# The gate of a recurrent block, computed by pairs of tokens

## The chip, the cores and the metric

One core of one Trainium2 chip runs the whole program. The metric is the time of one execution on the device in microseconds (us).

## The reference, cut to what matters

The input x has 4 sequences of 1024 tokens and 512 features. Four layers follow each other, each adding its result to x; all is fp32. The third layer is the one that changes:

```
x = x + L0(x)          # two-layer MLP with an expert's rows, hidden size 2048
x = x + L1(x)          # 512 x 512 weight picked per sequence
# L2
ctx[t]  = a * ctx[t-1] + x[t]                       # causal average, a is one number
wg      = sigmoid([x, ctx] @ Wg.T + bg)             # Wg = [W1, W2], each 512 x 512
gated   = x * wg
mod     = 0.5 + sigmoid(gelu(x @ Wn1.T + bn1) @ Wn2.T + bn2)        # 4 columns
traces  = causal averages of gated * mod[d], d = 0..3
gate    = sigmoid(sum_d(traces[d] * blend[d]) @ Wtemp.T + btemp)
soma    = gelu(x @ Wsoma.T + bsoma)
x = x + layernorm((soma * gate) @ Wout.T) * gamma + beta
x = x + L3(x)          # 512 x 512 weight picked per sequence
```

## The kernel before, in words

The tokens are cut into 8 tiles of 512 (two per sequence, t or i = 0..7), the features into 4 chunks of 128 partitions (c or m = 0..3). A tile lies with its features on the partitions and its tokens along them. Each fp32 operand of TensorE (PE) is split into a high part (rounded to fp32r by an ACT copy) and a low part (the rest, by a DVE subtraction); a product is three fp32r matmuls, hi x hi, hi x lo and lo x hi (`split_product`, L1441 to L1443), each with a weight load of its own.

The work has two halves. **The first half** (layers 0 and 1) goes by pairs p = 0..3 of tiles. In a unit (p, k), k = 0..7, the first matrix of the MLP is multiplied by seven Strassen products (P1, P5, P6, P2, P7, P4, P3 on PE, in this order), with fc2 products of earlier blocks between them. Products P1, P6, P7 and P4 share a bank: ACT copies it out after P1, P6 and P7 (`p1_of`, `u2_of` at L972, `u3_of`), and P7 waits for `u2_of`. At unit 1 the second tile of the pair before passes through layer 1, and in unit 2 DVE makes its low parts (`x2_lo`). After the eight units the second tile of the pair has 16 fc2 steps, j = 0..15; the hidden blocks come back from DRAM (`hb_lo`, `w2_lo` make their low parts). The 37 pieces of the later weights are split on the way and parked in DRAM. The result x2 of a tile is stored as fp32 and as its two parts.

**The second half** (layers 2 and 3) goes by tiles i. PE's order in round r from 2 on is: N1(r), the first gate block (r,0) with the small product MO(r) inside, TE of tile r-1 (four blocks), gates (r,1) and (r,2), L3 of tile r-2 (four blocks, in round 7 two), gate (r,3), OU of tile r-1, SO(r), with SS(r-1) between. Tile 0's gates lie between the last fc2 steps of the first half (after j = 4, 7, 10, 13), and in round 1 the gates (1,1), (1,2), (1,3) follow one another, since no L3 is ready.

A gate block (i, m) sums over eight products: because gate[t] - a gate[t-1] = (W1 + W2) x[t] - a W1 x[t-1], each chunk gives one product with W1 + W2 and one with -a W1 and the tokens moved by one (the tile is loaded behind a halo of one token, `LEAD`). DVE then runs the recurrence over the bank (`scan_g`, L2078), ACT takes the tanh (`wg_tanh`), and DVE makes `gated`, four drives, four traces and their sum (`traces_a` to `traces_d`) and its low part (`temporal_low`), which TE needs in the next round. The gate weights, 1 MB for each m, are loaded once and stay (`wg_hl[0..3]`).

Each engine runs an instruction list written out by hand; waits are on semaphores, and nothing is reordered. Loads and stores are issued from SP's queue, some from ACT's and POOL's, in the order of the code.

Of the kernel before, what the change touches and what calls it, by code (L numbers as in the profile page):

```python
# [23 lines left out]
SLOTS = 6  # L24

# [16 lines left out]
def build(nc, x, tok16, tok8, small, fc1_w, fc2_w, exp_w, exp_b, l1_w, l1_b, wg, wn1, wsoma, wtemp, wout,  # L42
# [15 lines left out]
    with ctx:  # L58
# [12 lines left out]
        def sem(name):  # L71
# [38 lines left out]
        mod_row = place("mod_row", 4, [TOK])  # L110

        LEAD = 64
        SLOT_KIB = 2 * (LEAD + TOK) * 4 / KIB
        x2_slot = [place(f"x2_slot{s}", 6 + SLOT_KIB * s if s < 4 else 112 + SLOT_KIB * (s - 4), [2, LEAD + TOK], F32R)
                   for s in range(SLOTS)]
        gated = place("gated", 24, [TOK])
        drive = [place(f"drive{s}", 26 + 2 * s, [TOK]) for s in range(2)]
        sumsq = place("sumsq", 30, [TOK])
        sumsq_lo = place("sumsq_lo", 30, [TOK], F32R)
        h1_hi = place("h1_hi", 30, [TOK], F32R)  # L120
        wg_hl = [place(f"wg_hl{m}", at, [2 * KC, 2, P], F32R) for m, at in enumerate((32, 56, 64, 72))]
        mod_t = place("mod_t", 40, [TAUS, TOK])
        temporal = place("temporal", 160, [KC, TOK])
        temporal_lo = place("temporal_lo", 160, [KC, TOK], F32R)
        wsoma_hl = place("wsoma_hl", 80, [KC, 2, DIM], F32R)
# [10 lines left out]
        l3w_at = (152, 156, 200, 121)  # L136
        l3w_hl = [place(f"l3w_hl{c}", at, [2, DIM], F32R) for c, at in enumerate(l3w_at)]

        l3w_last = [place(f"l3w_last{c}", at, [2, DIM], F32R) for c, at in enumerate((32, 36, 56, 60))]
        o_late = place("o_late", 64, [KC, TOK])  # L140
        x3_hi_late = place("x3_hi_late", 64, [KC, TOK], F32R)
        sq_late = place("sq_late", 72, [KC, TOK])
        spikes_hi_late = place("spikes_hi_late", 80, [KC, TOK], F32R)
        y_sb = [place("y_sb0", 125, [TOK]), place("y_sb1", 4, [TOK])]

        wn2_hl = place("wn2_hl", 127, [2, P], F32R)
# [10 lines left out]
        alpha_minus = const("alpha_minus", 1)  # L157
# [6 lines left out]
        zeros = const("zeros", 2)  # L164
        ones = const("ones", P, F32R)
        ident = const("ident", P)
# [40 lines left out]
        s_wg = [sem(f"s_wg{m}") for m in range(KC)]  # L207
# [18 lines left out]
        s_halo = [sem(f"s_halo{c}") for c in range(KC)]  # L226
        s_zero = sem("s_zero")
        s_last_hi = sem("s_last_hi")
        s_slot = [sem(f"s_slot{s}") for s in range(SLOTS)]
        s_xt = [sem(f"s_xt{s}") for s in range(3)]  # L230
# [6 lines left out]
                ("L1", "N1", "SO", "MO", "WG", "TE", "OU", "SS", "L3")}  # L237
# [154 lines left out]
        MADE = [p for p, (k, _) in enumerate(PARKED) if k in ("WG", "OU", "L3")]  # L392


        parked_units = ((4, 5, 6, 7, K8 + 3, K8 + 6, K8 + 9, K8 + 12),
                        (1, 2, 3, 5, 6, K8 + 4, K8 + 8, K8 + 12),
# [18 lines left out]
        for c in range(0, 2 * KC, 2):  # L415
            p = PARKED.index(("WG", c))
            assert parked_number[p + 1] == parked_number[p] + 1
# [51 lines left out]

        def x2_at(i, c):  # L470
            return (KC * i + c) % SLOTS
# [42 lines left out]
        def _(eng):  # L514
# [67 lines left out]
            def load_stage(n):  # L582
# [4 lines left out]
                else:  # L587
# [5 lines left out]
                    elif k == "WG":  # L593
                        source = wg[:, c // 2 if c % 2 else KC + c // 2, :]
# [9 lines left out]
            def parked(k, c):  # L604
# [3 lines left out]
                return parked_dram(p).rearrange("a p n -> p a n")  # L608
# [5 lines left out]
            def load_wg(m):  # L614
                if m:
# [4 lines left out]
                parked("WG", 2 * KC - 1)  # L620
                eng.dma_start(wg_hl[m].bitcast(F32).rearrange("p k a n -> p (k a) n"),
                              wg_dram[:, :, :, m * P:(m + 1) * P].rearrange("k a p n -> p (k a) n")
                              ).then_inc(s_wg[m], 16)

            def load_wsoma(c):
                if c < 2:
                    on.wait_ge(s_x2st, 16 * LAST)
                    on.wait_ge(s_x2lo, KC * LAST)
                on.wait_ge(s_stlo, STAGED)
                on.wait_ge(s_pstlo, 16 * len(PARKED))  # L630
                for row in range(2):
                    on.wait_ge(s_hbst[row], 16 * K8 * PAIRS)
# [10 lines left out]
            def load_x(t):  # L643
                if t >= 2:
                    on.wait_ge(s_x2st, 16 * (t - 1))
                    on.wait_ge(s_x2lo, KC * (t - 1))
# [12 lines left out]

            def load_xt(i):  # L660
# [4 lines left out]
                elif i == 2:  # L665
                    on.wait_ge(s_x2lo, KC * NT)
# [5 lines left out]
            def load_slot(i, c):  # L672
                if i == 0:
                    on.wait_ge(s_prod, prod_no(PAIRS - 1, K8 - 1, ("P6", "P2", "P7", "P4")[c]) + 1)
                elif c < 2:
                    if i > 1:
                        on.wait_ge(s_pe["SO"], KC * (i - 1))
                    else:
                        on.wait_ge(s_fc2, UNITS)
# [6 lines left out]
                if i % HALVES:  # L686
                    on.wait_ge(s_halo[c], 16 * (i // HALVES + 1))
                else:
                    on.wait_ge(s_zero, 16 * KC * B)
                s = x2_at(i, c)  # L690

                if c == KC - 1 and i > 1:
                    eng.dma_start(x2_slot[s][:, 0, LEAD - 1:].bitcast(F32), x2hl_dram[i, c, :, 0, :]).then_inc(s_last_hi, 16)
                    eng.dma_start(x2_slot[s][:, 1, LEAD - 1:].bitcast(F32), x2hl_dram[i, c, :, 1, :]).then_inc(s_slot[s], 16)
                else:
                    eng.dma_start(x2_slot[s][:, :, LEAD - 1:].bitcast(F32), x2hl_dram[i, c]).then_inc(s_slot[s], 16)

            def load_l3w(b):
                for c in range(KC):
                    if b == B - 1:  # L700
                        on.wait_ge(s_pe["WG"], KC * LAST + 1 + c // 2)
# [5 lines left out]
                    else:  # L707
                        on.wait_ge(s_fc2, UNITS)
                    eng.dma_start(l3w_of_tile(HALVES * b, c)[:, :, :].bitcast(F32), parked("L3", KC * b + c)).then_inc(s_l3w[c], 16)
# [23 lines left out]
            for p in range(PAIRS):  # L733
                for k in range(K8):
# [5 lines left out]
                    if p and k == 2:  # L740
                        store_x2(HALVES * p - 2)
                    if p and k == 4:
                        store_x2(HALVES * p - 1)
                    if k in (5, 6):
                        load_x(HALVES * p + k - 5)
# [3 lines left out]
                    if k == K8 - 1 and p == PAIRS - 1:  # L749
# [3 lines left out]
                        for c in range(1, KC):  # L753
                            load_slot(0, c)
                    store_hb(p, k, 1)
# [8 lines left out]
                for j in range(HC if p < PAIRS - 1 else 0):  # L764
                    pass_staged(p, K8 + j)
                    if j in (4, 8):
# [11 lines left out]
            uses_done(4)  # L778
            load_wg(2)
# [1795 lines left out]
```

## Time and profile before

| | |
|---|---|
| median of 2 runs | 1317.53 us (1317.52 to 1317.55) |
| profiled execution | 1317.3 us, of which the span of the trace is 1315.6 |
| PE | 1306.4 us busy, 5725 matmuls |
| DVE | 1033.5 us busy |
| ACT | 668.5 us busy |
| DMA | 196.57 MB, 149 GB/s on average |

The span is the time from the first to the last instruction of the program in the trace. PE's busy time counts a matmul from its start to a modelled end, and successive ones overlap: it tells that PE is hardly ever without work, not how fast it works. The time of a matmul in a stream is read from a stretch: its length divided by the matmuls that start in it.

### The profile page before, as it was taken

The numbers are of one execution on the slowest core, as the hardware profiler recorded it, in microseconds if no ns is written. First come the engines' busy times: TensorE is split into PE (matmuls) and PEld (weight loads), VectorE is DVE, ScalarE is ACT, GpSimd is POOL, SyncE is SP. The second block draws the span as 40 slices with busy tenths as digits, with TensorE's granted clock in tenths as the row PEclk, the third lists the DMA queues.
The fourth block names the chain that finished last, engine by engine and source line by source line (L and its number), as shares of the span: only waits on it lengthen the run. The fifth ranks groups of instructions, "written<-read, shape, count | busy, mean of one in ns | idle before, by whom it ended". The sixth has DMA issues, their size and how long they took to land.

```text
span 1315.6 us, 16412 instructions
## 1 busy us (share of the span) xinstructions
PE 1306.4 (99%) x5725; PEld 1072.1 (81%) x5725; DVE 1033.5 (79%) x1635; ACT 668.5 (51%) x1237; POOL 102.1 (8%) x135
## 2 busy tenths in 40 slices
PE   9999999999999999999999999999999999999998
PEld 7788888888888888888887887788888888888877
DVE  7876786767778768676644898999898889897974
ACT  6576475765466664566643322434334353535254
POOL 0010010030000000100000100013000210021000
PEclk9999999999999999999999999999999999999999
DMA  8256563766445766636667567512132123312101
GB/s 289 97 179 230 168 176 121 231 169 202 139 135 189 233 214 194 167 102 222 229 216 212 175 205 198 186 41 88 65 130 95 65 97 128 97 65 97 49 16 64
DMA packets 102122, 196.57 MB, mean 149 GB/s; under 512 B 9704, under 2 KB 28136, under 8 KB 98968
## 3 DMA queue, kind: packets, MB, share of 16 engines
q1 hardware_dynamic: 84608, 154.99, 37.1%
q10 hardware_dynamic: 11576, 24.70, 6.1%
q0 software_dynamic: 5856, 15.83, 3.9%
q8 instruction: 46, 0.75, 0.2%
q14 instruction: 36, 0.29, 0.1%
HBM read 125.65 MB, written 69.83 MB: 149 GB/s over the span
## 4 chain that ended last, share of the span: by engine, by line
PE 92%; DVE 5%; ACT 1%; issue 1%; DMA 0%; ACTq 0%; DVEq 0%
PE bank L1441 31%; PE bank L1442 30%; PE bank L1443 30%; DVE drive L2115 1%; DVE drive L2102 1%; DVE temporal L2130 0%; DVE t_lo L1876 0%; DMA x_raw<-in_x 0%; DVE temporal L2115 0%; DVE bank L2078 0%; ACT x_hl L1043 0%; DVE sp_hl L1876 0%; DVE t_raw L1905 0%; DVE w_hl L1876 0%; ACT bank L983 0%
## 5 line engine op out<-in xcount | busy, mean ns | idle before, releaser
L1441 PE MATMUL bank<-h_hl,w_hl 128*128 128x512 f32 x512 | 199.5, 390 | 0.0
L1443 PE MATMUL bank<-h_hl,w_hl 128*128 128x512 f32 x512 | 199.3, 389 | 0.0
L1442 PE MATMUL bank<-h_hl,w_hl 128*128 128x512 f32 x512 | 199.2, 389 | 0.0
L1441 PE MATMUL bank<-t_hi,sp_hl 128*128 128x512 f32 x448 | 175.3, 391 | 3.7 <-DVE t_lo L1876 1.2
L1442 PE MATMUL bank<-t_lo,sp_hl 128*128 128x512 f32 x448 | 174.4, 389 | 0.0
L1443 PE MATMUL bank<-t_hi,sp_hl 128*128 128x512 f32 x448 | 174.3, 389 | 0.0
L1441 PEld LDWEIGHTS bank<-h_hl,w_hl 128*128 128x128 f32 x512 | 96.1, 188 | 20.9 <-issue 0.8
L1443 PEld LDWEIGHTS bank<-h_hl,w_hl 128*128 128x128 f32 x512 | 96.1, 188 | 20.0
L1442 PEld LDWEIGHTS bank<-h_hl,w_hl 128*128 128x128 f32 x512 | 96.1, 188 | 19.8
L1441 PEld LDWEIGHTS bank<-t_hi,sp_hl 128*128 128x128 f32 x448 | 84.1, 188 | 24.4 <-issue 1.8
L1441 PE MATMUL bank<-x_slot,wg_hl 128*128 128x512 f32 x256 | 100.6, 393 | 0.0
L1442 PE MATMUL bank<-x_slot,wg_hl 128*128 128x512 f32 x256 | 99.8, 390 | 0.0
L1443 PE MATMUL bank<-x_slot,wg_hl 128*128 128x512 f32 x256 | 99.4, 388 | 0.0
L1443 PEld LDWEIGHTS bank<-t_hi,sp_hl 128*128 128x128 f32 x448 | 84.1, 188 | 17.5
L1442 PEld LDWEIGHTS bank<-t_lo,sp_hl 128*128 128x128 f32 x448 | 84.1, 188 | 17.2
L2102 DVE SCALAR_TENSOR_TENSOR drive<-gated,small_sb,mod_t 128x512 f32<-128x512 f32 x128 | 92.1, 740 | 3.7 <-issue 2.1
L1876 DVE TENSOR_TENSOR w_hl<-w_raw,w_hl 128x512 fp32r<-128x512 f32 x128 | 86.8, 686 | 6.5 <-ACT w_hl L959 5.4
L1026 ACT ACTIVATE h_hl<-hb_in 128x512 fp32r<-128x512 f32 x64 | 40.2, 628 | 87.3 <-DMA hb_in<-hb_dram 44.9
L959 ACT ACTIVATE w_hl<-w_raw 128x512 fp32r<-128x512 f32 x128 | 78.4, 620 | 6.3 <-PE bank L1443 6.3
L1876 DVE TENSOR_TENSOR h_hl<-hb_in,h_hl 128x512 fp32r<-128x512 f32 x64 | 44.0, 688 | 38.5 <-ACT h_hl L1026 38.5
L943 ACT ACTIVATE sp_hl<-s_raw_sb 128x256 fp32r<-128x256 f32 x128 | 50.9, 411 | 39.5 <-PE bank L1443 38.0
L2130 DVE TENSOR_TENSOR temporal<-drive,temporal 128x512 f32<-128x512 f32 x96 | 66.0, 687 | 1.0
(225 smaller groups left out, 2824.3 us busy)
## 6 DMA issues: line engine op xcount, KB each, us to landing
fc_raw<-in_fc_w SPq DMA_DIRECT2D x32, 512.0 KB, 4.2
hb_dram<-hb_out SPq DMA_DIRECT2D x64, 256.0 KB, 2.6
hb_in<-hb_dram ACTq DMA_DIRECT2D x64, 256.0 KB, 3.3
x2hl_dram<-x_hl POOLq DMA_DIRECT2D x28, 512.0 KB, 7.1
x_slot<-x2hl_dram SPq DMA_DIRECT2D x26, 513.0 KB, 5.1
stage<-in_l_w SPq DMA_DIRECT2D x32, 256.0 KB, 3.5
x_raw<-in_x SPq DMA_DIRECT2D x8, 1024.0 KB, 6.3
x_dram<-x_raw SPq DMA_DIRECT2D x8, 1024.0 KB, 8.1
```

Source lines behind the costliest of these rows:

```text
L943: eng.activation(sp_hl[n % RING][:, 0, :, :], product_source(n), ACT.Copy).then_inc(s_shi, 1)
L959: eng.activation(w2_hl[v % 3][:, 0, :, :], w2_raw[:, j, :, :], ACT.Copy).then_inc(s_w2hi, 1)
L1026: eng.activation(h_hl[v % 4][:, 0, :], hb_in[v % 4][:, :], ACT.Copy).then_inc(s_hhi, 1)
L1441: eng.matmul(ps, w_hi, x_hi, start=first, stop=False, skip_group_check=resumed)
L1442: eng.matmul(ps, w_hi, x_lo, start=False, stop=False, skip_group_check=resumed)
L1443: return eng.matmul(ps, w_lo, x_hi, start=False, stop=final, skip_group_check=resumed)
L1876: return eng.tensor_tensor(lo, raw, hi.bitcast(F32), ALU.subtract)
L2102: eng.scalar_tensor_tensor(drive[d % 2][:, :], gated[:, :], blend_sb[:, TAUS * c + d:TAUS * c + d + 1], mod_t[:, d, :], ALU.mult, ALU.mult ...
L2115: eng.tensor_tensor_scan(traced, alpha[:, 1 + d:2 + d].to_broadcast([P, TOK]), drive[d % 2][:, :], start, ALU.mult, ALU.add).then_inc(s_tr ...
L2130: eng.tensor_tensor(temporal[:, c, :], drive[d % 2][:, :], temporal[:, c, :], ALU.add).then_inc(s_add, 1)
```

## The change

The gate is computed by pairs of tokens 2k and 2k+1. With q[k] = W2 ctx[2k], the even token is W1 x[2k] + q[k], and the odd one (W1 + W2) x[2k+1] + a q[k]. A block is three products for each chunk, on 256 columns: q, even tokens, odd tokens, the moving operand taking every second word of a tile. The context is made by DVE scans in place over x2 and split into parts by ACT and DVE, and stored; for tiles 0 to 5 this lies in units 2 to 6 of the pair after, for tile 6 in steps j = 12 to 15, for tile 7 in round 1. ACT copies q out twice, once times a (`q_of`), and DVE adds it to the bank (`gate_sum`) where the scan was. The gate weights have 12 pieces (1.5 MB for each m) and two buffers: each block's weights are loaded anew, from block 6 on by ACT behind the tanh of two blocks earlier. The halo is gone. Tile 0's gates now lie after j = 4, 8, 11, 14. The places of tiles in SBUF and banks, and some waits, are moved to suit.

```diff
-        wg_hl = [place(f"wg_hl{m}", at, [2 * KC, 2, P], F32R) for m, at in enumerate((32, 56, 64, 72))]
+        wg_hl = [place(f"wg_hl{g}", at, [3 * KC, 2, P], F32R) for g, at in enumerate((28, 68))]
-        PARKED += [("WG", c) for c in range(2 * KC)]
-        PARKED += [("OU", c) for c in range(KC)] + [("L3", c) for c in range(B * KC)]
+        PARKED += [("WG", c) for c in range(3)] + [("OU", 0)] + [("WG", c) for c in range(3, 3 * KC)]
+        PARKED += [("OU", c) for c in range(1, KC)] + [("L3", c) for c in range(B * KC)]
...
+        def q_bank(i, m):
+            b, half = (((6, 1), (0, 0), (1, 0), (3, 0)) if i else ((6, 1), (4, 0), (5, 0), (4, 1)))[m]
+            return bank[b][:, PAIR * half:PAIR * (half + 1)]
...
+                if k == "WG":
+                    eng.dma_start(wg_dram[:, :, c, 0, :].rearrange("m p n -> p m n"),
+                                  stage_hi[:, :].bitcast(F32).rearrange("p (m n) -> p m n", n=P)).then_inc(s_psthi, 16)
...
+            def store_ctx(t):
+                on.wait_ge(s_ctxlo, KC * (t + 1))
+                eng.dma_start(ctx_dram[t], x_raw[t % 2][:, :, :]).then_inc(s_ctxst, 16)
...
+            def load_ctx(i, c):
+                if i:
+                    on.wait_ge(s_pe["WG"], KC * i)
...
+            def ctx_hi(t, c):
+                on.wait_ge(s_ctx, KC * t + c + 1)
+                if t % HALVES == 0:
+                    eng.activation(g_last[:, c:c + 1], x_raw[t % 2][:, c, TOK - 1:TOK], ACT.Copy).then_inc(s_glast, 1)
+                    on.wait_ge(s_glast, KC * (t // HALVES) + c + 1)
+                xc = pairs(x_raw[t % 2][:, c, :])
+                eng.activation(xc[:, :, 1].bitcast(F32R), xc[:, :, 0], ACT.Copy).then_inc(s_ctxhi, 1)
...
+            def q_of(i, m):
+                n = KC * i + m
+                on.wait_ge(s_pe["Q"], n + 1)
+                on.wait_ge(s_g, n)
+                eng.activation(q_sb[:, 0:PAIR], q_bank(i, m), ACT.Copy)
+                eng.activation(q_sb[:, PAIR:], q_bank(i, m), ACT.Copy, scale=alpha[:, 0:1]).then_inc(s_q, 1)
+
             def wg_tanh(i, m):
                 ps = wg_bank(i, m)
                 on.wait_ge(s_g, KC * i + m + 1)
...
                 eng.activation(ps[:, :], ps[:, :], ACT.Tanh, bias=bg_sb[:, m:m + 1], scale=0.5
                                ).then_inc(s_wgt, 1)
+                g = KC * i + m + 2
+                if 6 <= g < KC * NT:
+                    on.wait_ge(s_pe["WG"], g - 1)
+                    eng.dma_start(wg_hl[g % 2][:, :, :, :].bitcast(F32), wg_dram[g % KC]).then_inc(s_wg[g % 2], 16)
...
+            contexts_at = {3: (0, 0), 4: (0, 2), 5: (1, 0), 6: (1, 2)}
             def unit(p, k):                       # ACT
...
                     h_of_c12(p, k - 1)
                     staged_hi(p, k - 1, late=True)
+                    if p and k in contexts_at:
+                        ctx_hi(t - 1 + contexts_at[k][0], contexts_at[k][1])
+                        ctx_hi(t - 1 + contexts_at[k][0], contexts_at[k][1] + 1)
...
-                on.wait_ge(s_wg[m], 16)
+                g = KC * i + m
+                w = wg_hl[g % 2]
+                on.wait_ge(s_wg[g % 2], 16 * (g // 2 + 1))
+                if i == 0:
+                    on.wait_ge(s_x2 if m else s_x1, KC * LAST)
+                    if m == 3:
+                        on.wait_ge(s_q, 2)
+                elif m:
+                    on.wait_ge(s_spk, KC * (i - 1) + (1, 2, 4)[m - 1])
+                else:
+                    on.wait_ge(s_gated, KC * (i - 1) + (3 if i > 1 else 4))
+                if m == 0 and i:
+                    gate_tokens(i, m, 0, 1)
+                    if i == 2:
+                        mo(i)
+                on.wait_ge(s_cslot, 16 * KC * (i + 1))
+                for c in range(KC):
+                    mm = split_product(q_bank(i, m), w[:, 3 * c + 2, 0, :], w[:, 3 * c + 2, 1, :],
+                                       ctx_slot[c][:, :, 1], ctx_slot[c][:, :, 0], c == 0, c == KC - 1)
+                mm.then_inc(s_pe["Q"], 1)
+                if m == 0 and i > 2:
+                    mo(i)
+                if m or not i:
+                    gate_tokens(i, m, 0, 1)
+                gate_tokens(i, m, 1, 0).then_inc(s_pe["WG"], 1)
+
+            def gate_tokens(i, m, token, part):
+                w = wg_hl[(KC * i + m) % 2]
                 for c in range(KC):
                     x2 = slot(i, c)
-                    for k, before in ((2 * c, 0), (2 * c + 1, 1)):
-                        at = LEAD - before
-                        mm = split_product(wg_bank(i, m)[:, :], wg_hl[m][:, k, 0, :], wg_hl[m][:, k, 1, :],
-                                           x2[:, 0, at:at + TOK],
-                                           x2[:, 1, at:at + TOK], c == 0 and not before,
-                                           c == KC - 1 and before == 1)
+                    mm = split_product(wg_bank(i, m)[:, PAIR * token:PAIR * (token + 1)], w[:, 3 * c + part, 0, :],
+                                       w[:, 3 * c + part, 1, :], pairs(x2[:, 0, :])[:, :, token], pairs(x2[:, 1, :])[:, :, token],
+                                       c == 0, c == KC - 1)
+                return mm
...
+            def context(t, c):
+                start = 0.0
+                on.wait_ge(s_x2st, 16 * (t + 1))
+                on.wait_ge(s_x2lo, KC * t + c + 1)
...
+                xr = x_raw[t % 2][:, c, :]
+                eng.tensor_tensor_scan(xr, alpha[:, 0:1].to_broadcast([P, TOK]), xr, start, ALU.mult, ALU.add
+                                       ).then_inc(s_ctx, 1)
+            def context_lo(t, c):
+                on.wait_ge(s_ctxhi, KC * t + c + 1)
+                xc = pairs(x_raw[t % 2][:, c, :])
+                low_part(xc[:, :, 0].bitcast(F32R), xc[:, :, 0], xc[:, :, 1]).then_inc(s_ctxlo, 1)
-            def scan_g(i, m):
...
+            def gate_sum(i, m):
+                ps = wg_bank(i, m)
                 on.wait_ge(s_pe["WG"], KC * i + m + 1)
+                on.wait_ge(s_q, KC * i + m + 1)
+                eng.tensor_tensor(ps[:, :], ps[:, :], q_sb[:, :], ALU.add).then_inc(s_g, 1)
...
+            contexts_at = {2: (0, 0), 3: (0, 2), 4: (1, 0), 5: (1, 2)}
             def unit(p, k):                       # DVE
...
                 staged_lo(p, k)
+                if p and k - 1 in contexts_at:
+                    context_lo(t - 1 + contexts_at[k - 1][0], contexts_at[k - 1][1])
+                    context_lo(t - 1 + contexts_at[k - 1][0], contexts_at[k - 1][1] + 1)
...
                 staged_made(p, k, late=True)
+                if p and k in contexts_at:
+                    context(t - 1 + contexts_at[k][0], contexts_at[k][1])
+                    context(t - 1 + contexts_at[k][0], contexts_at[k][1] + 1)
...
                     if j == 12:
+                        context(LAST - 1, 0)
+                        context(LAST - 1, 1)
                         traces_a(0, 1)
                     if j == 13:
+                        context(LAST - 1, 2)
+                        context(LAST - 1, 3)
                         traces_b(0, 1)
                     if j == 14:
+                        context_lo(LAST - 1, 0)
+                        context_lo(LAST - 1, 1)
                         traces_c(0, 1)
+                        gate_sum(0, 2)
+                    if j == 15:
+                        context_lo(LAST - 1, 2)
+                        context_lo(LAST - 1, 3)
                         traces_d(0, 1)
...
             spikes_low(0, 2, 2)
+            context(LAST, 0)
+            context(LAST, 1)
             traces_d(1, 0)
-            scan_g(1, 1)
+            gate_sum(1, 1)
```

## Rows read from the trace of the kernel before

**Rows 1.** The page, part 1: busy us (share of the span) and instructions by engine.

```profile
PE 1306.4 (99%) x5725; PEld 1072.1 (81%) x5725; DVE 1033.5 (79%) x1635; ACT 668.5 (51%) x1237; POOL 102.1 (8%) x135
```

**Rows 2.** Stretches: length, then PE, PEld, DVE, ACT, POOL busy, PEclk, DMA, GB/s.

```profile
730.00:860.00 130.00, 129.50 (x561) 104.15 (x560) 122.32 (x169) 44.10 (x76) 5.83 (x9) 1.00 0.62 184
...
1058.25:1127.65 69.40, 69.40 (x306) 57.23 (x305) 62.43 (x76) 28.62 (x45) 0.71 (x1) 1.00 0.31 106
```

**Rows 3.** Stretches, PE alone: three gate blocks; two SO blocks.

```profile
809.65:826.11 16.46, 16.46 (x73) 1.00 0.99 185
...
837.01:842.45 5.44, 5.44 (x25) 1.00 0.01 3
```

**Rows 4.** Weight loads: timeline of the warm-up (start, length), and lines (busy, mean ns).

```profile
1.21 3.70 PEld L1751 LDWEIGHTS bank<-ones 128*128 128x128 f32 x17 [1.21 <-DVE eps_sb L2205]
...
5.10 0.53 PEld L1751 LDWEIGHTS bank<-ones 128*128 128x128 f32 x4
...
L1442 PEld LDWEIGHTS bank<-x_slot,wg_hl 128*128 128x128 f32 x256 | 48.0, 188 | 10.0
```

**Rows 5.** Lines by form, DVE and ACT: count, busy us, mean ns, idle before.

```profile
L2078 DVE TENSOR_TENSOR_SCAN bank<-alpha,g_last,bank 128x512 f32<-128x512 f32 x16 | 20.5, 1283 | 4.3 <-PE bank L1443 4.3
...
L1952 DVE TENSOR_TENSOR bank<-bank,p_sb 128x512 f32<-128x512 f32 x28 | 19.6, 698 | 21.6 <-PE bank L1443 21.6
...
L2115 DVE TENSOR_TENSOR_SCAN drive<-alpha,drive 128x512 f32<-128x512 f32 x48 | 58.1, 1210 | 0.0
...
L1876 DVE TENSOR_TENSOR sp_hl<-s_raw_sb,sp_hl 128x256 fp32r<-128x256 f32 x128 | 52.3, 420 | 17.5 <-ACT sp_hl L943 17.5
...
L943 ACT ACTIVATE sp_hl<-s_raw_sb 128x256 fp32r<-128x256 f32 x128 | 50.9, 411 | 39.5 <-PE bank L1443 38.0 <-DVE s_raw_sb L1919 1.3
```

**Rows 6.** Timeline (start us, us) of pair 3, unit 3 and the start of unit 4.

```profile
606.26 2.49 DVE L1876 TENSOR_TENSOR x_hl<-x_raw,x_hl 128x512 fp32r<-128x512 f32 x4
...
608.61 0.60 ACT L972 ACTIVATE u_sb<-bank 128x512 f32<-128x512 f32 x1 [0.38 <-PE bank L1443]
...
609.77 0.39 PE L1441 MATMUL bank<-t_hi,sp_hl 128*128 128x512 f32 x1
...
620.02 0.68 DVE L1876 TENSOR_TENSOR w_hl<-w_raw,w_hl 128x512 fp32r<-128x512 f32 x1
...
623.57 0.60 ACT L972 ACTIVATE u_sb<-bank 128x512 f32<-128x512 f32 x1 [0.38 <-PE bank L1443]
```

**Rows 7.** Timeline (start us, us) from step j = 14 to the start of TE(1).

```profile
757.88 0.69 DVE L1876 TENSOR_TENSOR w_hl<-w_raw,w_hl 128x512 fp32r<-128x512 f32 x1
...
762.11 0.40 PE L1441 MATMUL bank<-h_hl,w_hl 128*128 128x512 f32 x1
...
798.77 0.39 PE L1441 MATMUL bank<-ts_hi,wtemp_hl 128*128 128x512 f32 x1
...
820.78 1.29 DVE L2078 TENSOR_TENSOR_SCAN bank<-alpha,g_last,bank 128x512 f32<-128x512 f32 x1
...
826.12 0.40 PE L1441 MATMUL bank<-ts_hi,wout_hl 128*128 128x512 f32 x1
...
857.50 2.35 DVE L1876 TENSOR_TENSOR temporal_lo<-temporal,ts_hi 128x1024 fp32r<-128x1024 f32 x2
...
858.86 0.47 PE L1441 MATMUL bank<-ts_hi,wtemp_hl 128*128 128x512 f32 x1 [0.17 <-DVE temporal_lo L1876]
```

**Rows 8.** DMA issues of the whole span: count, KB each, median us to landing.

```profile
xt<-x_dram SPq DMA_DIRECT2D x8, 1024.0 KB, 5.8
```

**Rows 9.** Timeline (start us, us) of round 6, and of round 7 to TE(7).

```profile
1151.20 1.28 DVE L2165 SCALAR_TENSOR_TENSOR soma<-bank,soma 128x512 f32<-128x512 f32 x2
...
1224.96 1.28 DVE L2078 TENSOR_TENSOR_SCAN bank<-alpha,g_last,bank 128x512 f32<-128x512 f32 x1
...
1262.77 2.35 DVE L1876 TENSOR_TENSOR temporal_lo<-temporal,ts_hi 128x1024 fp32r<-128x1024 f32 x2
...
1264.59 0.39 PE L1441 MATMUL bank<-ts_hi,wtemp_hl 128*128 128x512 f32 x1
```

More of the change, by code:

```diff
@@ L206, in build @@
         s_wn1 = sem("s_wn1")
-        s_wg = [sem(f"s_wg{m}") for m in range(KC)]
+        s_wg = [sem(f"s_wg{g}") for g in range(2)]
         s_wsoma = sem("s_wsoma")
@@ L225, in build @@
         s_hl7 = [sem(f"s_hl7{c}") for c in range(KC)]
[L226 to L227 removed]
+        s_ctx = sem("s_ctx")
+        s_ctxhi = sem("s_ctxhi")
+        s_ctxlo = sem("s_ctxlo")
+        s_ctxst = sem("s_ctxst")
         s_last_hi = sem("s_last_hi")
         s_slot = [sem(f"s_slot{s}") for s in range(SLOTS)]
+        s_cslot = sem("s_cslot")
+        s_q = sem("s_q")
         s_xt = [sem(f"s_xt{s}") for s in range(3)]
@@ L414, in build @@
         STAGED = len(staging)
-        for c in range(0, 2 * KC, 2):
+        for c in range(0, 3 * KC, 3):
             p = PARKED.index(("WG", c))
@@ L619, in load_wg @@
                     on.wait_ge(s_prod, prod_no(PAIRS - 1, K8 - 1, "P6") + 1)
[L620 to L623, printed above, removed]
+                was_parked("WG", 3 * KC - 1)
+                eng.dma_start(wg_hl[g % 2][:, :, :, :].bitcast(F32), wg_dram[g % KC]).then_inc(s_wg[g % 2], 16)
             def load_wsoma(c):
[L626 to L632, printed above, removed]
+                on.wait_ge(s_w2lo, UNITS - HC + 2 * c + 2)
                 eng.dma_start(wsoma_hl[:, c, :, :].bitcast(F32), parked("SO", c)).then_inc(s_wsoma, 16)
@@ L678, in load_slot @@
                     else:
-                        on.wait_ge(s_fc2, UNITS)
+                        on.wait_ge(s_ctxst, 16 * LAST)
+                        for row in range(2):
+                            on.wait_ge(s_hbst[row], 16 * K8 * PAIRS)
+                        on.wait_ge(s_prod, len(PRODUCTS))
                 else:
@@ L708, in load_l3w @@
                         on.wait_ge(s_fc2, UNITS)
+                        on.wait_ge(s_stlo, STAGED)
+                        on.wait_ge(s_pstlo, 16 * len(PARKED))
+                        for row in range(2):
+                            on.wait_ge(s_hbst[row], 16 * K8 * PAIRS)
                     eng.dma_start(l3w_of_tile(HALVES * b, c)[:, :, :].bitcast(F32), parked("L3", KC * b + c)).then_inc(s_l3w[c], 16)
@@ L752, in _ @@
                         load_wg(0)
-                        for c in range(1, KC):
+                        for c in (1, 3, 2):
                             load_slot(0, c)
+                        for c in range(KC):
+                            load_ctx(0, c)
                     store_hb(p, k, 1)
@@ L823, in _ @@
                 if r + 1 < NT:
+                    for c in range(KC):
+                        load_ctx(r + 1, c)
                     load_slot(r + 1, 2)
@@ L1348, in _ @@
                 spikes_hi(0, m)
+            ctx_hi(LAST, 0)
+            ctx_hi(LAST, 1)
+            q_of(1, 1)
             wg_tanh(1, 1)
+            ctx_hi(LAST, 2)
+            ctx_hi(LAST, 3)
+            q_of(1, 2)
             wg_tanh(1, 2)
+            q_of(1, 3)
             for m in range(KC):
@@ L1380, in _ @@
                     te_tanh(r - 1, m)
-                for m in range(KC):
+                for m in range(SH):
                     spikes_hi(r - 1, m)
+                q_of(r, 1)
+                spikes_hi(r - 1, SH)
                 wg_tanh(r, 1)
+                q_of(r, 2)
                 y_of(r - 2, 0)
@@ L2408, in _ @@
             x2_of(LAST, 2)
-            scan_g(1, 0)
+            gate_sum(1, 0)
             x2_of(LAST, 3)
@@ L2430, in _ @@
             sum_squares(0)
-            scan_g(1, 3)
+            gate_sum(1, 3)
             traces_c(1, 2)
```

287 lines of the change are left out of this document (161 added, 126 removed).

## The prediction, made before the result was known

> **What bounds the kernel now.** I read the page's busy times first: PE is busy 99% of the span [rows 1]. The reader should see that nothing else can be the bound on average: every microsecond taken from PE shows, and every one that another engine adds shows only where PE comes to wait for it. Next I read stretches. In a round of the second half PE has 306 matmuls in 69.40 us and DVE 62.43 us of work; but from 730 to 860 us, where the last tiles of the first half and tiles 0 and 1 of the second overlap, DVE has 122.3 us in 130 [rows 2]. There DVE is all but a second bound, and the change adds work to it.
>
> **The gate product.** Now a gate block (tile, output block m) is 24 matmuls of 512 columns. Three blocks (72 matmuls; the count shown includes one that began earlier) take 16.46 us, 228.6 ns each, so a block is 5.49 us; beside it 24 matmuls of SO take 5.44 us, 226.7 ns each [rows 3]. The clock is granted in full, so 512 columns at 2.4 GHz are 213.3 ns, and 13.4 ns go to each matmul whatever its columns. The new block is 36 matmuls of 256 columns: 106.7 + 13.4 = 120.0 ns each, 4.32 us, 1.17 us less. Weights must keep up, one load for each matmul: a load is recorded with 188 ns, but in the warm-up, once the clock is up, four loads of 188 ns lie in 0.53 us, one every (0.53 - 0.19) / 3 = 0.113 us [rows 4]. So a 256-column matmul lies between 113 ns (loads bound) and 113 + 13.4 = 126 ns (the fixed part comes on top); 120 is between them and I take it: a block gains 0.95 to 1.42 us, 32 blocks 37 us if nothing else moves.
>
> The Trainium skill (TensorE: Matmul & The Clock Gate, Back-to-back issue gap) gives N/2.4 + 2.5 ns for one matmul after another, 109 ns for 256 columns and 216 for 512; the trace has 226.7 for 512, so I don't use it. By it the block would gain 1.56 us.
>
> The moving operand now takes every second fp32 word. No matmul of the trace does that. Bounds: no cost, or half rate, so that a matmul costs the 226.7 ns of a full one and a block 8.16 us, 2.67 more than now. The nearest row is the gate itself, which reads half its operands one word off: 2 ns a matmul [rows 3]. I take no cost; the other end is a rival.
> The Trainium skill (SBUF — State Buffer, Door 1: The DMA port swizzle, the note on cachelines) says that reads run at full rate with two hits in each 16-byte line, which two words apart in fp32 still has; no run here shows it.
>
> **DVE's part.** A scan in the bank (1.28 us) becomes an add (0.70) [rows 5]: 0.6 us less, 32 times. Added are 32 context scans (1.21 each, as the scan of the drive) and 32 low parts of 256 columns (0.42); ACT gets 32 high parts of 256 columns (0.41) and two short copies for each gate block. Stepped operands may cost DVE up to 0.4 us for each of 64 instructions (a 512-column instruction against 256) or nothing; I take nothing. Four more weight pieces are staged, 512-byte pieces in their stores: hidden, since SP's queue loads weights three units ahead. The dropped halo stores and the zero fills were off the path.
>
> **First half, units 3 to 6 of pairs 1 to 3.** Here I find the first new wait. ACT gets two `ctx_hi` near the start of a unit, ahead of `u2_of`; they wait for two context scans that DVE makes at the end of the unit before. PE's P7 waits for `u2_of`. In unit 3 of pair 3, DVE ends the four `x2_lo` at 606.26 + 2.49 = 608.75; `u2_of` ran at 608.61 to 609.21 and P7 began at 609.77 [rows 6], as soon as P2 was through. With the change the scans end at 608.75 + 2.42 = 611.2; then ACT has the second `ctx_hi` (0.4, and a one-column copy), `product_hi` 0.4, `w2_hi` and `u2_of` 0.6 each, `product_hi` 0.4, overlapping by a tenth: u2 is there at 613.5 and P7 is 3.7 us late. In units 4 to 6 the scans start when the low part of w at 620.02 is through, 620.6, and end at 623.0; u2 at 625.3 in place of 624.17 [rows 6], of which 0.56 was slack: 0.6 us. A pair loses 3.7 + 3 x 0.6 = 5.5, three pairs **16.5 us**. DVE itself has gaps for this work, so nothing else shifts. Bounds: 0, if ACT's other work were ready, which its order excludes, to 22 with the stepped scans and copies at their worst.
>
> **The transition, to the start of TE(1).** In DVE's order, ahead of the low part for fc2 of j = 14, which ended at 757.88 + 0.69 = 758.57, come four contexts (+4.84); one scan turns to an add (-0.6), another moves behind (-1.13), and everything starts 1.16 earlier: 760.5. PE would want it at 762.11 - 5.49 (gate 3 moves behind) - 3 x 1.17 = 753.1 [rows 7]: 7.4 us of stall. The x1 of tile 7, for which `so_pair(0)` waits, is late by another 1.6 (two adds and four low parts lie ahead). So TE(0) starts at 798.77 + 9.0 - 5 x 1.17 = 801.9, 3.1 late although five gates are shorter.
> Then weights: only two gate buffers are left, and the load for block (1,3) is issued by ACT after tanh(1,1), which waits for `gate_sum(1,1)`, in the place of the scan at 820.78 [rows 7]: 820.78 + 3.1 + two contexts 2.5 + add 0.6 + tanh 0.7 = 827.7. A 1 MB load lands in 5.8 us [rows 8]; for 1.5 MB I take 7 (6 to 8.7): 834.7. PE has done (1,1) and (1,2) by 801.9 + 10.9 + 8.6 = 821.4 and waits 13.3 us; before, the three blocks ran through. OU(0), at 826.12 in the trace, starts at 839.0. Gate (2,0) is 1.17 shorter, so TE(1), at 858.86, comes at 870.6 by PE; by DVE, which must wait for the squares of OU(0), some 871. **+12.5 us** (8 to 20; all nine gates up to there are counted in it). In the trace TE(1) already waited for `temporal_lo`, which ended at 857.50 + 2.35 [rows 7].
>
> **Rounds 2 to 7.** From TE(1) on, 23 gate blocks remain: -26.9. DVE loses 4 x 0.6 of its 62.4 us and still fits 64.7. Block (r,2) now waits for the spikes of a bank that holds its context product: the first of the two spikes at 1151.20 [rows 9] ends at 1151.9, and gate (r,1) at 1151.75: 0.2 us a round, 1.2 in six. In round 7 only two L3 blocks, not four, lie between gates (7,2) and (7,3): the weights of (7,3) are asked for after the add in the place of the scan at 1224.96 [rows 9] and the tanh, and land 0.6 + 0.7 + 7 later, at 1233.3; PE began that gate 5.49 and 114 matmuls of 0.2267 ahead of TE(7), at 1233.3, and now comes at 1233.3 - 2.34 + 0.2 = 1231.1: 2.1 of stall. DVE would be late next: `temporal_lo` ended at 1265.12, 0.8 before the third chunk of TE(7), which started at 1264.59 [rows 9]; with PE held up that suffices. **-23.6** (-17 to -30).
>
> **Sum.** Against the profiled execution (span 1315.6 and 1.7 around it, 1317.3; 0.2 under the median): 1317.3 + 16.5 + 12.5 - 23.6 = 1322.7. I forecast **1323**, no change within 2%, its own range 1305 to 1344.
>
> **Rivals.**
> 1. *The waits don't bite* (0.13). PE is all that counts, and contexts and weights fit into gaps: 32 x 1.17 = 37 less, 1280; with some of the transition lost, 1290. For it: PE is busy 99% [rows 1], DVE in first-half units has gaps. Against it: the orders of ACT and DVE in the code, and the edge at TE(1) in rows 7. It decides if `u2_of` still ends before P7 and PE waits less than 3 us for weights in tile 1.
> 2. *Half rate for the stepped moving operand* (0.09). Place: the 1152 gate matmuls; price 2.67 us a block, 85 us in 32; DVE's waits vanish beside it in the transition but not in the units: 1317 + 85 + 11 = about 1413. It decides from 150 ns a matmul (5.4 us a block) on, where the gain is gone. Against it only the small price of the offset.
> 3. *The waits are deeper* (0.10). PE's clock: the first 17 weight loads came at 0.22 us each, half of full speed (1.2 GHz), after nothing had run, over 3.7 us [rows 4]; in the rest of the trace PE is never idle long and the clock stays at 1.00. If the stalls of 3.7 and 13 us drop it, each of the four costs half of 3.7 more, 7 us; with the units at 22, the transition at 20 (its loads queue behind each other) and the rounds at -17: 1317 + 22 + 20 - 17 + 7 = 1349. It decides when the clock row shows under 1.00 after a stall.
>    The Trainium skill (TensorE: Matmul & The Clock Gate, HAM oscillation) says that waits between bursts throttle the clock again; no row shows such a wait.
> 4. *The matmul isn't shortened* (0.03): if a load needed its whole 188 ns, 36 x 0.2 = 7.2 us a block, 55 more: about 1390. Rows 4 speak against it.
>
> **Numbers.** 2% is 26 us, about what one can tell from no change here: 1291 and 1344. The forecast (0.65) lies within them, its upper edge just touching. Faster 0.13, same 0.67, slower 0.20. Leaving out rivals 2 and 4 and the far ends of 1 and 3 gives 1290 to 1352.
>
> **What would show it.** Gate matmuls start every 120 ns; P7 in unit 3 of pairs 1 to 3 waits 3 to 4 us for `u_sb`; PE idles over 8 us before gate (1,3), for wg_hl; a round is 64.5 to 65 us; the clock stays 1.00 or dips after that gap. Wrong if PE's busy share is still 99%, or if gate matmuls come every 200 ns or more.

## The result: 9.5% slower

| | before | changed |
|---|---|---|
| median of 2 runs | 1317.53 us | 1442.85 us (1441.48 to 1444.21) |
| ratio | | 1.095 (1.090 to 1.100) |
| span of the trace | 1315.6 us | 1442.5 us |
| PE busy, matmuls | 1306.4 us, 5725 | 1410.5 us, 6109 |

The forecast was 1323, the range 1290 to 1352. The first view is the page's busy times, to be held against [rows 1]; the second is the costliest groups of the changed kernel, one shape a line (busy us, mean ns of one instruction, idle time before it and what ended it).

```profile
PE 1410.5 (98%) x6109; PEld 1173.1 (81%) x6109; DVE 1065.8 (74%) x1698; ACT 703.8 (49%) x1337; POOL 78.6 (5%) x102
```

```profile
L1537 PE MATMUL bank<-t_hi,sp_hl 128*128 128x512 f32 x448 | 178.4, 398 | 17.4 <-ACT u_sb L1017 14.0 <-DVE u_sb L2060 1.0 <-DVE t_lo L2003 0.9
...
L1537 PE MATMUL bank<-x_slot,wg_hl 128*128 128x256 f32 x256 | 104.8, 409 | 0.0
...
L1537 PE MATMUL bank<-x_slot,wsoma_hl 128*128 128x512 f32 x128 | 50.3, 393 | 0.0
```

PE is still the bound and still busy, so the time is not one large wait. The last two lines say where it went: a gate matmul of 256 columns is recorded with 409 ns, one of SO with twice the columns with 393. The first line holds the waits that I had expected in units 3 to 6: 14.0 us for `u_sb`, where the trace of before has none of this kind.

The stretches (PE alone; three windows) answer to [rows 3] and to the round of [rows 2]: gates (4,1) and (4,2), two blocks of SO, and a round.

```profile
1013.16:1029.69 16.53, 16.53 (x73) 1.00 0.26 96
1059.78:1065.22 5.44, 5.44 (x25) 1.00 0.32 133
1002.24:1082.80 80.56, 80.56 (x354) 1.00 0.49 183
```

Two gate blocks have 72 matmuls in 16.53 us: 229.6 ns each, where I had 120. A block takes 8.27 us instead of 5.49, at full clock and with no idle time. SO is unchanged at 226.7 ns. A round is 80.56 us, 11.2 more than before: four blocks by 2.78.

The first matmuls of five stages in each trace add the whole difference up (us from the start of the span; the two columns at the right are runs 2 and 9 below):

| starts | before | changed | words side by side | last version |
|---|---|---|---|---|
| N1(0) | 695.45 | 729.52 | 727.57 | 700.76 |
| TE(0) | 798.77 | 846.74 | 834.51 | 808.86 |
| TE(1) | 858.86 | 921.67 | 904.04 | 872.42 |
| TE(7) | 1264.59 | 1391.57 | 1288.82 | 1253.58 |
| end | 1315.61 | 1442.53 | 1339.99 | 1305.19 |

Of the 126.9 us, 34.1 are lost ahead of N1(0); 13.9 to TE(0) (five gates by 2.78: 13.9); 14.8 to TE(1) (four gates: 11.1, and a wait of 4.0 for weights); 64.2 to TE(7) (23 gates: 63.9). After TE(7) nothing changes. So the gates are 32 x 2.78 = 89 us, the first half is 34, and the weights are 4.

### The profile page after: what moved, and what is told of

Its sections match the earlier page's. It is cut to its first block, busy times and chain, and to the rows that moved or that the text cites. A ratio compares the mean times of both kernels' runs of the same rounds, so it can differ in the third digit from the quotient of the medians.

```text
span 1442.5 us, 17453 instructions
## 1 busy us (share of the span) xinstructions
PE 1410.5 (98%) x6109; PEld 1173.1 (81%) x6109; DVE 1065.8 (74%) x1698; ACT 703.8 (49%) x1337; POOL 78.6 (5%) x102
## 4 chain that ended last, share of the span: by engine, by line
PE 84%; DVE 9%; ACT 3%; DMA 3%; issue 2%; ACTq 0%; DVEq 0%
PE bank L1537 28%; PE bank L1538 27%; PE bank L1539 27%; DVE x_raw L2202 2%; DMA hb_in<-hb_dram 1%; DVE w_hl L2003 1%; DVE h_hl L2003 1%; ACT sp_hl L988 1%; DVE x_hl L2003 1%; DVE hb_out L2097 1%; DMA stage<-in_wg 1%; DVE x_raw L2154 1%; DVE sp_hl L2003 0%; DVE t_lo L2003 0%; ACT w_hl L1004 0%
## 5 line engine op out<-in xcount | busy, mean ns | idle before, releaser
L1537 PE MATMUL bank<-h_hl,w_hl 128*128 128x512 f32 x512 | 202.3, 395 | 5.6 <-DVE w_hl L2003 4.4
L1538 PE MATMUL bank<-h_hl,w_hl 128*128 128x512 f32 x512 | 201.1, 393 | 0.0
L1539 PE MATMUL bank<-h_hl,w_hl 128*128 128x512 f32 x512 | 200.9, 392 | 0.0
L1537 PE MATMUL bank<-t_hi,sp_hl 128*128 128x512 f32 x448 | 178.4, 398 | 17.4 <-ACT u_sb L1017 14.0
L1539 PE MATMUL bank<-t_hi,sp_hl 128*128 128x512 f32 x448 | 175.8, 392 | 0.0
L1537 PEld LDWEIGHTS bank<-h_hl,w_hl 128*128 128x128 f32 x512 | 97.6, 191 | 29.5 <-DVE h_hl L2003 7.5
L1539 PEld LDWEIGHTS bank<-h_hl,w_hl 128*128 128x128 f32 x512 | 97.3, 190 | 20.7
L1538 PEld LDWEIGHTS bank<-h_hl,w_hl 128*128 128x128 f32 x512 | 97.5, 190 | 20.1
L1539 PE MATMUL bank<-x_slot,wg_hl 128*128 128x256 f32 x256 | 104.9, 410 | 0.0
L1538 PE MATMUL bank<-x_slot,wg_hl 128*128 128x256 f32 x256 | 104.9, 410 | 0.0
L1537 PE MATMUL bank<-x_slot,wg_hl 128*128 128x256 f32 x256 | 104.8, 409 | 0.0
```

The lines of the kernel that those rows point to most:

```text
L1537: eng.matmul(ps, w_hi, x_hi, start=first, stop=False, skip_group_check=resumed)
L1538: eng.matmul(ps, w_hi, x_lo, start=False, stop=False, skip_group_check=resumed)
L1539: return eng.matmul(ps, w_lo, x_hi, start=False, stop=final, skip_group_check=resumed)
```

## The experiments

Theories: **step** (reading every second word costs PE the time of the words skipped), against **size** (256 columns cost some 230 ns however they lie) and **load** (the weight load, recorded with 209 ns beside the gate, doesn't let matmuls come closer). For the first half: the waits for the context's high parts and the clock after them, against other waits taking their place.

**1. The forms of a read, in the kernel before.**

```diff
+ if m == 0: return [(whole, lambda x: x.rearrange("p (k a) -> p a k", a=2))]
+ if m == 1: return [(lower, lambda x: x[:, lower]), (upper, lambda x: x[:, upper])]
+ if m == 2: return [(lower, lambda x: x.rearrange("p (k a) -> p k a", a=2)[:, :, 0]), ...]
+ if i % 2: return [(whole, lambda x: x.rearrange("p (k a) -> p a k", a=4))]
+ return [(whole, lambda x: x.rearrange("p (k a b) -> p a k b", a=2, b=2))]
```

> The kernel before, with the gate's moving operand read in other ways; what is computed is no longer the gate. Block m = 0: 512 columns in two sweeps of every second word. m = 1: each matmul split into two of 256 neighbouring words. m = 2: split into two of 256 columns, every second word. m = 3: 512 columns, in odd tiles in four sweeps of every fourth word, in even tiles in two sweeps of runs of two words. Step theory (every second word is read at half rate): m = 0 about 450 ns a matmul, m = 1 about 120, m = 2 about 230, m = 3 from 450 (or 900) in odd tiles; runs of two words may cost nothing or the same 450. Rival, size theory (256 columns cost 230 ns in whatever order): m = 0 227, m = 1 and m = 2 both 230, m = 3 227. Rival, load theory (no matmul comes closer than its weight load of 190 to 209 ns allows): m = 0 227, m = 1 and m = 2 both 200 to 230.

Four stretches, PE alone: block (2,1), 48 matmuls of 256 words side by side; (2,2), 48 of 256 stepped by two; (2,3), 24 of 512 in runs of two; (3,3), 24 of 512 by every fourth word.

```profile
907.68:913.31 5.63, 5.63 (x50) 1.00 0.01 3
913.31:924.21 10.90, 10.90 (x50) 1.00 0.00 0
935.14:945.97 10.83, 10.83 (x25) 1.00 0.37 121
1020.90:1031.90 11.00, 11.00 (x25) 1.00 0.85 295
```

Divided by their matmuls: 117 ns side by side, 227 stepped, 451 in runs of two, 458 by every fourth. The 512 columns of m = 0 take 451 ns as well. Size and load fall: 256 columns do come every 117 ns, with a weight load each. Step stands, but not by the words skipped, since every fourth word costs no more than every second.

**2. The changed kernel with neighbouring words.**

```diff
...
- pairs(x2[:, 0, :])[:, :, token], pairs(x2[:, 1, :])[:, :, token],
+ x2[:, 0, PAIR * token:PAIR * (token + 1)], x2[:, 1, PAIR * token:PAIR * (token + 1)],
- ctx_slot[c][:, :, 1], ctx_slot[c][:, :, 0],
+ ctx_slot[c][:, 1, :], ctx_slot[c][:, 0, :],
```

> The changed kernel with the gate's 36 matmuls a block reading 256 neighbouring words (the first or the last half of a tile) in place of every second one, so the wrong tokens. Step theory: about 120 ns a matmul in place of 229.6, a block 4.3 us in place of 8.3; the 32 blocks give 126 us back, less the waits for weights and contexts that the slow blocks had covered (transition and rounds, 10 to 25 us): 1325 to 1345. Size or load theory: 229 ns a matmul still, 1438 to 1445.

1340.55 us, ratio to before 1.0175 (1.016 to 1.019): 102 us less than the changed kernel. A round (PE alone), and PE's longest wait between 860 and 870 us, ahead of gate (1,3):

```profile
984.90:1050.40 65.50, 64.99 (x353) 1.00 0.61 225
```

```profile
PE bank L1537 <- issue: 11.9, 1, 11.9
```

Within a gate block matmuls start every 120.0 ns, and the waits that the slow blocks had covered come out: 1.9 and 4.5 us in fc2's steps 14 and 15, 11.9 us for the weights of gate (1,3) (4.0 in the changed kernel), some 0.8 us in each round.

**3. The context's high parts moved behind `u2_of`.**

```diff
                     staged_hi(p, k - 1, late=True)
-                    if p and k in contexts_at: ctx_hi(...); ctx_hi(...)
...
                 staged_hi(p, k)
+                if p and k in contexts_at: ctx_hi(...); ctx_hi(...)
```

> The changed kernel with ACT's two context high parts of units 3 to 6 moved from ahead of the copy that P7 waits for to behind the unit's own high part of the staged weight. If these waits cost what I had worked out (5.5 us a pair) and the clock's fall after each 3.8 us stall another 1.4 to 2.8: 15 to 24 us less than the changed kernel, 1419 to 1428. If PE would find another wait in their place: under 5 us less.

1420.47 us: 22 less, the span 24.1 less, all of it ahead of N1(0) (705.48). First, the changed kernel in unit 3 of pair 3: the end of DVE's contexts, then ACT's chain from the context parts to `u_sb`, then PE's wait, then three stretches (PE alone).

```profile
631.50 2.33 DVE L2202 TENSOR_TENSOR_SCAN x_raw<-alpha,x_raw 128x512 f32<-128x512 f32 x2
```

```profile
632.98 0.43 ACT L1102 ACTIVATE x_raw<-x_raw 128x256 fp32r<-128x256 f32 x1
...
634.10 0.43 ACT L1102 ACTIVATE x_raw<-x_raw 128x256 fp32r<-128x256 f32 x1
...
635.56 0.58 ACT L1017 ACTIVATE u_sb<-bank 128x512 f32<-128x512 f32 x1
```

```profile
PE bank L1537 <- ACT u_sb L1017: 3.4, 1, 3.4
```

```profile
626.00:632.00 6.00, 6.00 (x28) 1.00 0.51 178
632.00:637.00 5.00, 1.56 (x6) 0.82 0.96 366
637.00:642.00 5.00, 5.00 (x13) 0.50 0.02 8
```

And the same place with the parts moved:

```profile
620.00:642.00 22.00, 21.78 (x97) 1.00 0.66 215
```

In the fences the scans end at 633.8, `u_sb` follows 2.3 us later, and P7 with it. Then comes what I had priced only in a rival: after these 3.6 us without work the granted clock is 0.50 (1.2 GHz), and 12 matmuls start in 5 us (the count shown includes one that began earlier) where 22 would. The waits sum to 15.9 us by their gaps (5.2, 5.2 and 5.5 a pair, each less a matmul's 227 ns). The matmuls behind the three long waits, held against 227 ns each, lost 1.5, 2.9 and 2.9 us more: 7.2. The two make 23.1 of the 24.1 that the edit brought; the last us is what is left of smaller waits, some of which went while others came.

**4. Both edits** (the diffs of runs 2 and 3).

> Both edits, neighbouring words (wrong tokens) and the later context high parts. Step theory: 1303 to 1328, that is the part of the prediction that is left when the waits of units 3 to 6 are gone; size or load theory: 1419 to 1428, as the later parts alone.

1319.83 us, ratio 1.0018 (1.0009 to 1.0028). What keeps this kernel from being faster than before is the transition (12.5 us from N1(0) to TE(1)), and some 10 us ahead of N1(0) that neither edit touches.

**5. The full computation with the parts stored evens first**, the later high parts of run 3, and the contexts made and stored a unit later.

```diff
- eng.activation(x_hl[:, 0, c, :], x_raw[t % 2][:, c, :], ACT.Copy).then_inc(s_x2hi, 1)
+ eng.activation(halved(x_hl[:, 0, c, :]), swept(x_raw[t % 2][:, c, :]), ACT.Copy).then_inc(s_x2hi, 1)
- eng.activation(soma[:, m, :], so_bank(m)[:, :], ACT.Gelu, ...)
+ eng.activation(swept(soma[:, m, :]), halved(so_bank(m)[:, :]), ACT.Gelu, ...)
- eng.tensor_tensor_scan(xr, alpha[:, 0:1].to_broadcast([P, TOK]), xr, start, ...)
+ eng.tensor_tensor_scan(ctx_sb[:, c, :], alpha[:, 0:1].to_broadcast([P, TOK]), xr, start, ...)
```

(Shown are the lines that reorder. `swept` reads a row as "p (k a) -> p a k", `halved` as "p (a k) -> p a k"; h1, the low parts and the context's parts likewise.)

> The gate by pairs computed in full, with the parts of x2 and of the context stored evens first, so that every gate matmul reads 256 neighbouring words; ACT and DVE do the reordering (x2's parts, the gelu of N1 and of SO, the context's parts, which go through the free high parts of x), and the context parts are made a unit later and behind the copy that P7 waits for. Step theory: 117 to 120 ns a gate matmul, and the time of the run with neighbouring words and late context parts, 1319.8, plus what the stepped ACT and DVE instructions cost on the path: 1316 to 1330. Rival (stepped reads slow ACT and DVE as they slow PE, 0.6 us for each of 64 high parts, gelus and low parts): 1335 to 1350, since DVE is the bound in the transition.

1319.59 us, ratio 1.0007 (0.9998 to 1.0017): as run 4, so the reordering costs nothing that shows. ACT's stepped instructions grew by 0.03 to 0.04 us (gelu of SO 719 ns against 687 before, x2's high part 662 against 620), DVE's low parts not at all (684 against 686). The rival, that stepping slows these engines as it slows PE, falls.

**6. Three waits mended**, on run 5.

```diff
- if 6 <= g < KC * NT:                       # ACT, behind wg_tanh
+ if 6 <= g < KC * NT - 1 and g != 7:        # and load_wg(7), load_wg(31) on SP
...
- x3_low(r - 2, 0, 2); x3_low(r - 2, 2, 2); traces_b(r, 0); spikes(r - 1, 1)
+ spikes(r - 1, 1); x3_low(r - 2, 0, 2); x3_low(r - 2, 2, 2); traces_b(r, 0)
...
- K8 + 3, K8 + 6, K8 + 9, K8 + 12     # pair 1; pair 0's line stands with run 7
+ K8 + 2, K8 + 5, K8 + 8, K8 + 12
```

> As the one before, with three waits of the change mended: the gate weights of blocks (1,3) and (7,3) are asked for by SP when the buffer is free and not by ACT behind a tanh; the second product of spikes stands ahead of x3's low parts, so that gate (r,2) finds its bank free; and the staged weight pieces ahead of the two stalls of 1.8 and 2.2 us in the first half stand three fc2 steps ahead and not two. By the gaps of the run with neighbouring words and late parts: 12.1 us before gate (1,3) fall to about 3, the 0.9 us a round go, the stalls at 177 and 365 us go: 13 to 17 us less than the run before this, 1303 to 1315, faster than the kernel before by up to 1%. Rival (PE meets another wait of DVE in their place): 1314 to 1322.

1317.31 us, ratio 0.9987 (0.998 to 0.9996): hardly a gain; most of what I expected moved. PE's waits between 820 and 880 us:

```profile
PE bank L1548 <- issue: 6.5, 1, 6.5
PE bank L1548 <- DMA x_slot<-x2hl_dram: 3.7, 1, 3.7
```

The rounds' 0.8 us are gone, but the weights, asked for at 826.5 us (837.2 in run 5), take 10.7 us to land and the slots for N1(2) then come late: between 812 and 826 us and again from 850 on the DMA share is 1.0.

**7. The staging alone**, on run 3 (pair 0's line here, pair 1's as in run 6).

```diff
...
- K8 + 2, K8 + 4, K8 + 6, K8 + 8, K8 + 10, K8 + 12
+ K8 + 1, K8 + 3, K8 + 5, K8 + 7, K8 + 9, K8 + 12
```

> The changed kernel with the later context high parts and, as its only other edit, the staged weight pieces of the first half set three fc2 steps apart, not two, ahead of the pieces that must wait for their neighbour. If the stalls at 177 and 365 us (2.1 and 0.9 us with the parts late, and a cold clock behind the first) come from this staging, they go: 3 to 5 us less than the run with the later parts alone (1420.5), 1415.5 to 1417.5. If they come from the rest of the first half's DMA traffic: no change.

1422.28 us, no gain over run 3. The two stalls that I meant, at 177 and 365 us, did go, but a third took their place, at 146 us. First the changed kernel: SP's queue, then DVE, which waits for a weight piece.

```profile
169.23 0.33 SPq L593 DMA_DIRECT2D wtemp_dram<-stage_lo  x1
171.51 0.33 SPq L619 DMA_DIRECT2D stage<-in_wg  x1
```

```profile
174.92 0.69 DVE L2120 TENSOR_TENSOR stage<-stage,stage 128x512 f32<-128x512 f32 x1 [2.17 <-DMA stage<-in_wg]
```

Run 7, PE's waits from 140 to 180 us:

```profile
PE bank L1537 <- DVE w_hl L2003: 4.3, 1, 4.3
```

A gate piece needs its neighbour, whose load waits for the store of the piece two before; DVE stands still for it, and fc2's low parts with it. Where pieces come every second step this bites at 177 and 373 us. My new spacing had put one behind the loads of the next pair's x.

**8. How long must a run be?** Step alone didn't explain every fourth word.

```diff
+ run = ((4, 8, 16, 32), (64, 128, 256, 1))[i % 2][m]      # 256: in order; 1: every eighth word
+ return [(slice(0, TOK), lambda x: x.rearrange("p (k a b) -> p a k b", a=2, b=run))]
```

> The kernel before with the gate's moving operand in two sweeps of runs of 4, 8, 16 and 32 words (even tiles, m = 0 to 3), of 64 and 128 words, in order, and in eight sweeps of every eighth word (odd tiles); what is computed is no longer the gate. If the loss is of reads that aren't next to each other, runs of 4 or 8 come near 227 ns a matmul and every eighth word stays at 452. If it is of any operand with more than one loop, all but the one in order take 452.

The start of gate (4,0), runs of 4 words: the times of the matmuls of the first weight pair, of which three read from the tile's first word and three one word ahead of it.

```profile
1012.36 0.39 PE L1441 MATMUL bank<-x_slot,wg_hl 128*128 128x512 f32 x1
1012.59 0.40 PE L1442 MATMUL bank<-x_slot,wg_hl 128*128 128x512 f32 x1
1012.83 0.39 PE L1443 MATMUL bank<-x_slot,wg_hl 128*128 128x512 f32 x1
1013.05 0.65 PE L1441 MATMUL bank<-x_slot,wg_hl 128*128 128x512 f32 x1
1013.52 0.64 PE L1442 MATMUL bank<-x_slot,wg_hl 128*128 128x512 f32 x1
1013.98 0.63 PE L1443 MATMUL bank<-x_slot,wg_hl 128*128 128x512 f32 x1
1014.44 0.41 PE L1441 MATMUL bank<-x_slot,wg_hl 128*128 128x512 f32 x1
```

Runs of four from the first word come every 0.23 us; the same runs one word off every 0.46. Off by one, runs of 8, 16, 32, 64 and 128 take 325, 281, 260, 241 and 236 ns, every eighth word 431. All of it fits one reading to within 4%, at full clock: 16 bytes that lie on a 16-byte boundary (the tile's first word does) and are read whole go at a column per cycle, every other word at half of that (off by one a run loses its four outer words: for 16, 213.3 x 20 / 16 + 13.4 = 280).

The half is not a fixed number of PE's cycles, as two stretches show. The changed kernel and run 2 both wait for the weights of gate (1,3), and the granted clock behind the wait is 0.50 (1.2 GHz). PE alone in that gate, the changed kernel, then run 2:

```profile
878.94:883.94 5.00, 5.00 (x23) 0.50 0.42 157
866.62:871.96 5.34, 5.34 (x27) 0.50 0.49 169
```

From start to start 21 stepped matmuls take 5.00 us, 238 ns each, against 229.6 at full clock; 25 of neighbouring words take 5.34, 214 ns each, against 120. So at half the clock a stepped column takes little more than one cycle, and the changed kernel loses almost nothing by the slow clock there. What in the chip does this, no run shows.

**9. The staging and the loads' order once more**, the rest as in run 6.

```diff
- K8 + 10, K8 + 12),  ...  K8 + 9, K8 + 12),        # as in the changed kernel
+ K8 + 10, K8 + 13),  ...  K8 + 9, K8 + 13),
...
+ load_wg(7)
  load_slot(2, 0)
  load_slot(2, 1)
  store_ctx(LAST)
  load_xt(2)
- load_l3w(0)                                       # now behind load_slot(2, 3)
```

> The tuned version once more, with two of its edits made differently: the staged weight pieces stand as in the changed kernel, only the last of pairs 0 and 1 comes one fc2 step later (the other spacing had put a piece behind the first fc2 step, where it waited for 4.6 to 4.8 us); and SP asks for the gate weights of block (1,3) ahead of tile 2's slots and for the first weights of L3 behind them, since in the tuned run these weights took 10.8 us to land and the slots then came 4.0 us late for N1(2). If the staging costs its waits by where the pieces stand, the stalls at 146, 177 and 366 us are all under 1 us (4.8 less than the tuned run); if the loads' order decides, the 6.8 us before gate (1,3) and the 4.0 us in N1(2) fall by 3 to 6 together: 1307 to 1313 in all. Rival (DMA and DVE are both full between 812 and 872 us, DMA share 0.79 to 1.03, so an order only moves the wait): 1311 to 1315, from the staging alone.

1306.87 us, ratio 0.9913 (0.9899 to 0.9926): 0.9% faster than the kernel before. Before gate (1,3) PE waits 4.0 us, in N1(2) 0.4; the stalls at 146, 177 and 366 us are all gone; two of 0.7 and 0.8 us, behind late `hb_in`, have come at 506 and 510 us, and one of 1.3 us, for DVE's squares of OU(0), at 856 us. A round, and the longest wait between 820 and 870 us:

```profile
1002.26:1067.02 64.76, 64.76 (x355) 1.00 0.54 195
```

```profile
PE bank L1549 <- issue: 4.0, 1, 4.0
```

What stays are 6.5 us in fc2's steps 14 and 15, where DVE is busy 57.2 of the 58 us from 745 to 803.

## Why the prediction was wrong, step by step

**The step that failed** is the one on the stepped operand: "I take no cost; the other end is a rival." At full clock it costs half the rate. A block takes 8.27 us, not 4.32, and with the words side by side it takes 36 x 120.0 ns, so the rest of that step (13.4 ns a matmul, loads that keep up) was right. Rival 2 had the price (2.67 us a block; 2.78 was measured) and the place; I gave it 0.09 and left it out of the range. Its total, 1413, was still 30 short: beside the gates it had 11 us, where 38 were lost (34 ahead of N1(0), 4 for weights). The reason was a wrong nearest row: an operand one word off [rows 3] is read in whole lines but for its two ends, so its 2 ns say nothing of a step. With no row of its own, an operation that every one of 1152 matmuls uses should have kept both ends at even chances. The Trainium skill (SBUF — State Buffer, Door 1: The DMA port swizzle, the note on cachelines) pointed the same way as my choice, with two hits in each 16-byte line for full rate; for PE's fp32r reads the runs differ: two words of each line take 451 ns for 512 columns, all four 227, and the measurement decides.

**Units 3 to 6.** Right in mechanism and size: 5.2 to 5.5 us a pair against 5.5. Not counted were the 7.2 us of clock behind the waits, which stood in rival 3 alone. The Trainium skill (TensorE: Matmul & The Clock Gate, HAM oscillation) says that waits between bursts throttle the clock again, and the stretch at 0.50 agrees.

**Staging, "hidden".** Wrong: runs 7 and 9 show waits of some 4 us that come and go with the places of the pieces. The smaller stalls at 541, 720 and 727 us (0.5 to 1.3 us; at 541 and 720 `hb_in` landing 7 to 8 us after its issue) are put down to DMA traffic by the trace alone; no run took it away, and run 9 still starts N1(0) 5.3 us later than the kernel before.

**Transition and rounds.** Covered by slow gates in the changed kernel, but run 2 lays them bare. Up to TE(0) it loses 3.6 us (worked out: 3.1), with stalls of 1.9 and 4.5 where I had 7.4; from there to TE(1) 9.4 (worked out: 12.5 - 3.1 = 9.4), with 11.9 for the weights where I had 13.3. (The start that I had for TE(1), 871, is 12.1 behind 858.86 and not 12.5.) From TE(1) to TE(7) it gains 20.9 (worked out: 23.6): the bank of gate (r,2) comes free 0.8 us late and not 0.2, since the second product of spikes, not the first, is what it waits for.

**The sum.** Without the failed step the forecast of 1323 would have met 1340.55: some 18 us short, nearly all of it ahead of N1(0) (32.1 us lost there, 16.5 worked out), by the clock, the staging and those smaller stalls.

## What to carry to other kernels

Lay fp32r operands of TensorE so that each matmul reads whole, aligned 16-byte lines; let ACT or DVE reorder in a pass that they make anyway. Price an access pattern that no row shows by both ends, and ask whether the nearest row differs in the property that matters. A PE stall can cost more than itself, so look at the granted clock behind it: the stalls of 3.6 us lost 1.5 to 2.9 us more in slow matmuls. Of two stalls of 2 us near 175 us, the changed kernel's was followed by a clock of 0.50 (1.7 us more) and run 2's, of 2.2 us, was not.

## What was not expected of the hardware

- PE's reads: every second, fourth or eighth word cost nearly the same (451, 458 and 431 ns for 512 columns), and runs of four depend on where they start (230 or 455 ns).
- At a granted clock of 0.50 a stepped matmul of 256 columns takes 238 ns, hardly more than the 229.6 at full clock, while one of neighbouring words goes from 120 to 214.
- The recorded time of one weight load rises from 188 to 209 ns beside stepped reads and is 195 beside 256 neighbouring words, which still came every 120 ns.
- ACT's stepped copies and gelus cost 5% to 7% more, DVE's stepped low parts nothing.
